# Early-fusion block on one Trainium2 core: when the softmax sums, the context and the o weights are loaded, and who scales the context

## The reference, cut to what matters

```python
def _chunk_decompose(x2d):            # chunks of 64 tokens
    ch_bias = (max + min) / 2         # per chunk and channel
    xz = xp - ch_bias
    scale = per chunk and channel, from the chunk's and the channel's max
    result = clip(round(xz / s), -8, 7) * s

attn = einsum('bqhd,bkhd->bhqk', Q, K)          # 32 heads of 16
ctx = einsum('bhqk,bkhd->bqhd', softmax(attn), V)
r2, cb2 = _chunk_decompose(ctx)
h = h + (r2 @ WO + cb2 @ o_weight.T + o_bias)
logits = layernorm(h) @ gate_w.T + gate_b       # top 2 of 8 experts
h = h + experts(layernorm(h), routing)
```

## Time and profile before

| | us |
|---|---|
| median of 3 runs | 1689.76 |
| range of the runs | 1685.97 to 1696.05 |
| profiled execution | 1692.25 |
| its span | 1690.4 |
| PE busy | 1264.5 (75%) |
| DVE busy | 1221.0 (72%) |
| ACT busy | 846.1 (50%) |
| POOL busy | 448.7 (27%) |

### The profile page before, as it was taken

How to read it: one execution, slowest core, us unless ns; L and a number is a source line. 1 busy time by engine, 2 the same in 40 slices (tenths; PEclk the granted TensorE clock), 3 DMA queues, 4 the chain that set the end, 5 groups by cost and what they waited for, 6 DMA issues and landing times. The chain is left out here.

```text
span 1690.4 us, 30070 instructions
## 1 busy us (share of the span) xinstructions
PE 1264.5 (75%) x10051; PEld 729.9 (43%) x10170; DVE 1221.0 (72%) x2030; ACT 846.1 (50%) x1748; POOL 448.7 (27%) x277
## 2 busy tenths in 40 slices
PE   0257347637989999999999886225819999999993
PEld 0245213212334444444444332003817777777772
DVE  7985999977778888888888787368474555555551
ACT  3665413321667777777777656914203444444441
POOL 4000307662234333443330003010012333333311
PEclk9968669875999999999999988556558999999997
DMA  4000206679367776677755553373229999999965
GB/s 157 0 1 4 88 0 204 217 217 208 101 177 193 198 208 190 186 194 204 212 128 100 91 140 125 76 147 126 93 106 353 314 311 306 308 306 311 308 208 143
DMA packets 115112, 294.08 MB, mean 174 GB/s; under 512 B 19971, under 2 KB 54787, under 8 KB 104641
## 3 DMA queue, kind: packets, MB, share of 16 engines
q1 hardware_dynamic: 90280, 209.27, 40.9%
q0 software_dynamic: 23712, 81.28, 18.0%
q10 hardware_dynamic: 1056, 2.79, 0.5%
HBM read 208.03 MB, written 90.32 MB: 176 GB/s over the span
## 5 line engine op out<-in xcount | busy, mean ns | idle before, releaser
L1447 ACT ACTIVATE pT<-p 128x512 f32<-128x512 f32 x800 | 422.0, 608 | 188.5 <-PE p L1340 115.3
L1412 DVE TENSOR_REDUCE mxa<-p 128x1 f32<-128x512 f32 x640 | 409.6, 682 | 104.8 <-PE p L1322 104.2
L1322 PE MATMUL p<-ks,qs 96*128 96x512 bf16 x640 | 254.4, 401 | 49.0 <-DMA vs<-d_v 31.0
L1340 PE MATMUL p<-qs,ks 128*128 128x512 bf16 x560 | 216.3, 387 | 30.4 <-DMA qs<-nmT 18.5
L1358 PE MATMUL p<-pT,vs 128*32 128x128 f32 (+1 forms) x2560 | 207.3, 442 | 1.4 <-ACT pT L1447 1.4
L2083 POOL DMA_INDIRECT d_acc<-yo,slot_row x47 | 74.6, 1587 | 268.1 <-DVE yo L2231 249.4
L2113 PE MATMUL p<-x,w 128*128 128x256 bf16 (+1 forms) x1728 | 145.5, 246 | 0.0
L2113 PEld LDWEIGHTS p<-x,w 128*128 128x128 bf16 x1728 | 133.6, 98 | 13.8
L1358 PEld LDWEIGHTS p<-pT,vs 128*32 128x32 f32 x2560 | 67.1, 109 | 153.4 <-issue 109.4
L1322 PEld LDWEIGHTS p<-ks,qs 96*128 96x128 bf16 x640 | 62.3, 98 | 153.7 <-DVE mxa L1412 58.9
L1290 POOL CAST xT<-xT 128x2048 bf16<-128x2048 f32 x24 | 45.3, 1886 | 305.5 <-PE p L1358 293.3
(11 more groups left out here) (405 smaller groups left out, 2090.4 us busy)
## 6 DMA issues: line engine op xcount, KB each, us to landing
w<-d_w SPq DMA_DIRECT2D x18, 2048.0 KB, 9.4
d_w<-xT POOLq DMA_DIRECT2D x24, 1024.0 KB, 6.5
shared<-d_w SPq DMA_DIRECT2D x10, 2048.0 KB, 7.8
w<-d_w SPq DMA_DIRECT2D x18, 1024.0 KB, 10.9
xT<-in_w1T POOLq DMA_DIRECT2D x16, 1024.0 KB, 10.7
qs<-d_q SPq DMA_DIRECT2D x192, 80.0 KB, 3.6
ks<-d_k SPq DMA_DIRECT2D x192, 80.0 KB, 3.7
d_v<-xT SPq DMA_DIRECT2D x20, 512.0 KB, 4.4
```

What stands on the lines that cost most here:

```text
L1322: mm = pe.matmul(out, qs[u][0:STACK, h, q], ks[u][0:STACK, h, 0:512], start=True, stop=True)
L1340: mm = pe.matmul(out, ks[u][:, h, k], qs[u][:, h, 0:512], start=True, stop=True)
L1412: dve.tensor_reduce(mxa[u][:, h, qt:qt + 1], bank, AX.X, ALU.max, negate=True).then_inc(s_mfree, 1)
L1447: act.activation(dst, ps[:, second_bank(c, s)], ACT.Exp).then_inc(s_p, 1)
```

## The change

In `attend`, SyncE's loop is one iteration shorter and the last looped iteration is written out: the loads of the sums, contexts and inverses, and the store of the inverses, stand between its steps. The reciprocal of the sums stands behind the maxima of group 26. The o weights and the o bias are loaded in attend (`load_o`), in the space of the first q and k buffers, after the second pass of group 28. In `route`, the late reciprocal stands ahead of the quantization of batch 0, and `put_bias(0)` ahead of the load of the late inverses. ScalarE no longer scales; VectorE's `apply` does it for every batch. The order of TensorE's and VectorE's parts is changed.

```diff
+        first_q, first_k = (sb(f"{n}s0", [P, 4, T], BF16, c=middle) for n in "qk")
+        wTo = [x[:].rearrange("p h t -> p (h t)").bitcast(F32)[:, 0:IT // 2 * L].rearrange("p (i o) -> p i o", o=L)
+               for x in (first_q, first_k)]
+        bias_o = sb("bias_o", [EARLY * (T // CHUNK), L], c=middle)
+        def load_o(sp):
+            rows = a["o_wT"].rearrange("(i p) o -> p i o", p=P)
+            for k in range(2):
+                sp.dma_start(wTo[k], rows[:, k * IT // 2:(k + 1) * IT // 2]).then_inc(s_oin, 16)
+            sp.dma_start(bias_o[:], a["L0_attn_o_bias"].partition_broadcast(EARLY * (T // CHUNK))).then_inc(s_oin, 16)
...
-            with sp.Fori(0, NI - 1) as i:
+            def step(i, c):
+                store(i, c - 1)
+                sp.wait_ge(s_s, U2 * num(i, c))
+                sp.wait_ge(s_pv, KT * num(i, c) + 1)
+                load(i, c + R - 1)
+
+            with sp.Fori(0, NI - 2) as i:
                 for c in range(1, R + 1):
-                    store(i, c - 1)
-                    sp.wait_ge(s_s, U2 * num(i, c))
-                    sp.wait_ge(s_pv, KT * num(i, c) + 1)
-                    load(i, c + R - 1)
+                    step(i, c)
...
-            for u in range(2):
-                sp.wait_ge(s_wst[u], 16 * 3 * EXP_N // 2)
-                sp.wait_ge(s_ost[u], 8 * EARLY * HEADS // GH + 1)
-            sp.dma_start(sums[0:EARLY * HEADS], heads[0:EARLY * HEADS, HD]).then_inc(s_sumin, 16)
-            for b in range(EARLY):
-                load_context(sp, b)
-            sp.wait_ge(s_rs, 1)
-            sp.dma_start(d_sum[0:EARLY * HEADS], sums[0:EARLY * HEADS]).then_inc(s_rout, 16)
-            sp.wait_ge(s_rout, 16)
-            for b in range(2):
-                load_inverses(sp, b)
+            for c in range(1, R + 1):
+                step(NI - 2, c)
+                if c == 1:
+                    for u in range(2):
+                        sp.wait_ge(s_ost[u], 8 * EARLY * HEADS // GH + 1)
+                    sp.dma_start(sums[0:EARLY * HEADS], heads[0:EARLY * HEADS, HD]).then_inc(s_sumin, 16)
+                elif c == 2:
+                    sp.wait_ge(s_rs, 1)
+                    sp.dma_start(d_sum[0:EARLY * HEADS], sums[0:EARLY * HEADS]).then_inc(s_rout, 16)
+                    for u in range(2):
+                        sp.wait_ge(s_wst[u], 16 * 3 * EXP_N // 2)
+                    load_context(sp, 0)
+                elif c == 3:
+                    sp.wait_ge(s_rout, 16)
+                    load_inverses(sp, 0)
+                    load_context(sp, 1)
+                    load_inverses(sp, 1)
+                else:
+                    load_context(sp, 2)
+                    sp.wait_ge(s_den, 1)
+                    load_inverses(sp, 2)
             for c in range(1, R + 1):
                 store(NI - 1, c - 1)
                 if c == 1:
-                    sp.wait_ge(s_den, 1)
-                    load_inverses(sp, 2)
+                    sp.wait_ge(s_s, U2 * num(NI - 1, 1))
+                    load_o(sp)
...
-            with dve.Fori(0, NI - 1) as i:
+            with dve.Fori(0, NI - 2) as i:
                 for c in range(R):
                     maxima(i, c)
             for c in range(R):
-                maxima(NI - 1, c)
-                if c == 1:
+                maxima(NI - 2, c)
+                if c == 2:
                     dve.wait_ge(s_sumin, 16)
                     dve.reciprocal(sums[0:EARLY * HEADS], sums[0:EARLY * HEADS]).then_inc(s_rs, 1)
+            for c in range(R):
+                maxima(NI - 1, c)
...
             store_late_inverses(sp)
+            put_bias(0)
             sp.wait_ge(s_rout, 16 + 16 * LATE_PARTS)
             load_inverses(sp, EARLY)
-            put_bias(0)
...
             centre(1)
-            scale(1)
             centre(2)
-            scale(2)
             deviations(0)
             centre(3)
-            scale(3)
-            copy_turned(0)
...
             rows(1)
+            gates(0)
             rows(2)
-            gates(0)
+            gates(1)
             rows(3)
-            gates(1)
             gates(2)
             gates(3)
...
             def quantized(b):
                 q, k = group(b)
-                at = q.columns(k)
-                flat = xT[:, b].rearrange("p i t -> p (i t)")
-                dve.wait_ge(s_scaled[b], 1)
+                dve.wait_ge(s_centred[b], 1)
                 if b >= 2:
                     dve.wait_ge(s_omm, COMPS * (b - 1))
-                chain(dve.tensor_scalar(flat, flat, MAGIC, QMAX, ALU.subtract, ALU.min))
-                dve.tensor_tensor(q.chunks(qF[:, b % 2]), q.chunks(xT[:, b]), q.spread(q.F[:, :, at]), ALU.mult).then_inc(s_q, 1)
+                q.apply(dve, chain, k, xT[:, b], qF[:, b % 2], s_q)
...
-            chain(dve.memset(magic[:], MAGIC))
             prepare(0, quant, range(EARLY))
+            dve.wait_ge(s_sumin, 16 + 16 * LATE_PARTS)
+            dve.reciprocal(late[:], late[:]).then_inc(s_rs, 1)
             dve.wait_ge(s_centred[0], 1)
             quant.apply(dve, chain, 0, xT[:, 0], qF[:, 0], s_q)
-            dve.wait_ge(s_sumin, 16 + 16 * LATE_PARTS)
-            dve.reciprocal(late[:], late[:]).then_inc(s_rs, 1)
             residual(0)
+            variances(0)
             dve.wait_ge(s_ctx[EARLY], 16 * 2 * IT)
             chain(dve.tensor_tensor(xT[:, EARLY], xT[:, EARLY], den[:, EARLY % 2], ALU.mult))
             last.extremes(dve, chain, 0, xT[:, EARLY])
+            normed(0)
             dve.wait_ge(last.bias_ready, 1)
             prepare(1, last, [EARLY])
-            variances(0)
             quantized(1)
             residual(1)
+            quantized(2)
             variances(1)
-            normed(0)
-            quantized(2)
+            normed(1)
             residual(2)
+            quantized(3)
             variances(2)
-            normed(1)
-            quantized(3)
+            normed(2)
             residual(3)
             variances(3)
-            normed(2)
             normed(3)
```

More of the change, by code:

```diff
@@ L172, in early_fusion_kernel @@
         heads = d_o.rearrange("g (h r) t -> (g h) r t", r=32)
+        first_q, first_k = (sb(f"{n}s0", [P, 4, T], BF16, c=middle) for n in "qk")
+        wTo = [x[:].rearrange("p h t -> p (h t)").bitcast(F32)[:, 0:IT // 2 * L].rearrange("p (i o) -> p i o", o=L)
+               for x in (first_q, first_k)]
+        bias_o = sb("bias_o", [EARLY * (T // CHUNK), L], c=middle)
+        s_oin = ctx.enter_context(nc.semaphore("o_inputs_in"))
+        def load_o(sp):
[3 more added lines that the diff above has]
+            sp.dma_start(bias_o[:], a["L0_attn_o_bias"].partition_broadcast(EARLY * (T // CHUNK))).then_inc(s_oin, 16)
         def load_late_sums(sp):
@@ L856, in apply, with round @@
     def apply(self, dve, chain, b, x, out, done):
+        x4 = self.chunks(x)
+        chain(dve.tensor_tensor(x4, x4, self.spread(self.s[:, :, self.columns(b)]), ALU.mult))
+        self.round(dve, chain, b, x, out, done)
+    def round(self, dve, chain, b, x, out, done):
         at = self.columns(b)
@@ L860, in apply @@
         flat = x.rearrange("p i t -> p (i t)")
-        chain(dve.tensor_tensor(x4, x4, self.spread(self.s[:, :, at]), ALU.mult))
         chain(dve.tensor_scalar(flat, flat, MAGIC, MAGIC, ALU.add, ALU.subtract))
@@ L1143, in attend @@
     d_w, xT4, den, quant, s_ctx, s_den, s_centred = (g[n] for n in ("d_w", "xT4", "den", "quant", "s_ctx", "s_den", "s_centred"))
-    load_late_sums = g["load_late_sums"]
+    load_late_sums, load_o = g["load_late_sums"], g["load_o"]
     GH = 4
@@ L1170, in sem @@
             return ctx.enter_context(nc.semaphore(name))
-        qs = [sb(f"qs{u}", [P, GH, T], BF16) for u in range(R)]
-        ks = [sb(f"ks{u}", [P, GH, T], BF16) for u in range(R)]
+        qs = [g["first_q"]] + [sb(f"qs{u}", [P, GH, T], BF16) for u in range(1, R)]
+        ks = [g["first_k"]] + [sb(f"ks{u}", [P, GH, T], BF16) for u in range(1, R)]
         vs = [sb(f"vs{u}", [P, KT, GH * 32]) for u in range(R)]
@@ L1524, in route @@
     s_ctx, s_sumin, s_rs, s_rout, s_centred = (g[n] for n in ("s_ctx", "s_sumin", "s_rs", "s_rout", "s_centred"))
-    load_inverses, store_late_inverses = g["load_inverses"], g["store_late_inverses"]
+    load_inverses, store_late_inverses, wTo, bias, s_oin = (g[n] for n in (
+        "load_inverses", "store_late_inverses", "wTo", "bias_o", "s_oin"))
     LATE_PARTS = T // LATE_COLS
@@ L1538, in route @@
         qF = sb("qF4", [P, 2, IT, T], BF16)
-        wTo = sb("wTo", [P, IT, L])
-        bias = sb("bias_o", [NE, L])
         Bt = [sb("Bt_early", [NE, L]), sb("Bt_last", [NB, L])]
-        magic = sb("magic4", [P, 1])
         gtok = sb("gtok4", [P, TILES])
@@ L1588, in route @@
         s_unit = sem("unit_experts_ready")
-        s_in, s_rin = sem("o_inputs_in"), sem("router_inputs_in")
+        s_rin = sem("router_inputs_in")
         c_dve = sem("p4_dve_chain")
```

(22 more changed lines are left out.)

## The result

| | before | after |
|---|---|---|
| median, us | 1691.78 (4 runs) | 1669.68 (4 runs) |
| range, us | 1685.97 to 1696.05 | 1667.11 to 1670.49 |
| profiled execution, its span | 1692.25, 1690.4 | 1667.11, 1665.3 |

Forecast were 1673 and the range 1658 to 1687.

A forecast was written before the change was run, and what follows sets the result against it. The prediction took TensorE's chain through the expert stage, fed by VectorE's routing, as the bound. Attention +10, t0 -24 and rest of the block -5 made -19 us: 1692.25 to 1673.3, said as 1673, range 1658 to 1687.

The forecast's parts named there:

- attention: Segment from the end of group 26's maxima to the route block: forecast 10 us longer.
- t0: VectorE's first addition into hs; from the route block's start to it, forecast 24 us less, bounds 18 to 28.
- The sums' stall: In attention, VectorE's wait for the sums moves from behind group 29's maxima to group 26's: 0 us.
- Rival B: In attention, the sums come before VectorE asks, giving up to 8.2 us: 1665 us, chance 0.06.
- Load 31: Last q/k load in attention, queued behind inverses and context 1; TensorE stands 8 to 11 us, 10 taken, bounds 0 and 23.
- Rival A: In attention, load 31 comes in time on idle engines with smaller spill: 1663 us, chance 0.17.
- Bt_early: In routing, VectorE starts it 8.5 us earlier, with o weights and bias loaded ahead; bounds 8 to 9.5.
- The first addition into hs: In routing, the accumulation's 11.4 us grows by 0 to 6, 4 taken, with batch 3's inverses running beside it.
- Rival D: In routing, GpSimd's descriptors or shared engines hold the accumulation 12 us more: 1685 us, chance 0.12.
- idle of 8 to 11 us: Sign of a right forecast: TensorE or VectorE idles on a DMA at the start of group 31's scores.
- VectorE's scaling: In routing, VectorE's scaling adds 2.95 us for each of three batches, 8.9 us on the bound engine.
- The order of parts: From t0 to the logits, reordered quantize, residual, normed and gates, scaling included: 5 us less, bounds 0 to 8.

The follow-up runs named there:

- a3: Changed kernel with the early reciprocal of the sums behind the maxima of group 27 instead of 26: 1662.27 us, ratio 0.9819 to before.
- a1: Changed kernel with attention's old schedule of loads and sums' reciprocal, o weights still loaded in attention: 1668.43 us, ratio 0.9865 to before.
- a2: Kernel before with only attention's new schedule, routing as before and o weights loaded there: 1693.22 us, ratio 0.9998 to before.
- b4: Changed kernel with inverses 0 and 1 and contexts 1 and 2 issued behind load 31: 1673.96 us, ratio 0.9891 to before.
- c0: Changed kernel with GpSimd's three products waiting for VectorE's joined maxima of groups 29, 30 and 31: 1670.06 us, ratio 0.9872 to before.
- b1: Changed kernel with batch 3's inverses loaded only after the first two accumulations into hs have landed: 1675.31 us, ratio 0.9911 to before.
- c1: Changed kernel, batch 3's inverses behind the first two hs accumulations, GpSimd's accumulations of batches 1 to 3 behind those inverses: 1662.76 us, ratio 0.9826.
- b2: Changed kernel with Bt_early written behind the late inverses again: 1673.01 us, ratio 0.9896 to before.
- b3: Changed kernel with ScalarE scaling batches 1 to 3 again, in the new order of parts: 1661.04 us, ratio 0.9826 to before.

## Why the prediction was right, and where a term was not

The time came out in the range, 3 us below the forecast, and the sum of the three segments as forecast. Two terms were off in opposite directions, attention by 4.7 us and t0 by 5.2, and they cancelled: that the sum is so close is luck.

**The sums' stall: right.** It moved and did not shrink (8.06 us), as the equal phase of store and maxima said. Rival B is refuted by the row, though a3 shows that it was one line away.

**Load 31: the mechanism right, the size wrong.** This is the first step that failed: "It ends at about C26 + 41. Load 31 waits behind them and lands some 8 to 11 us later". The copy of group 26 began at 952.98. GpSimd's second product, released by inverses 1, starts at 992.89 = C26 + 39.9, so the transfers ahead ended about when forecast. But load 31's v landed at 982.48 + 16.9 = 999.4, C26 + 46.4: 6.5 us behind them, and not 8 to 11. And it was needed later than C26 + 41.5, at about C28 + 4 = 998.3 (the copy of 28 at 994.34), C26 + 45.4, since the groups between had slipped too. The stall was 1.38 us where 10 stood in the sum. That load 31 did not pass is plain from the landing: v took 4.5 and 4.8 us in the last two loads of before, 5.3 and 5.0 in loads 28 and 30 of after, and 16.9 behind the inverses. The Trainium skill, "DMA: Bandwidth & Descriptors", section on queues, rings and completion order, says that each engine takes its own ring in order; this landing agrees. Part of the lateness came before the queue: inverses 1 held SyncE for 8.42 us, so store 27 was issued at 975.01, 2.5 us behind the end of its copy. Rival A was nearly right that load 31 costs little, but for the wrong reason: nothing passed on idle engines.

**The rest of attention's slip: not foreseen.** The segment grew by 5.3 us (a1 and a2 give 4.0 and 5.9). The steps between the ends of the `nm` additions tell where, held against 18.5 to 18.9 us for a step of before without a stall. In after the step with the stall is 1.1 us shorter than before's; the steps to groups 28, 29, 30 and 31 are longer by 0.6, 2.6, 1.4 and 3.1; and from group 31 to the block it is 1.3 shorter. The 2.6 us are the held addition of group 29, the 1.4 are TensorE's wait for load 31, and 1.5 of the 3.1 are the held addition of group 31; the rest stays open. Taking away the wait (b4) or the held additions (c0) gave nothing: in b4 an addition was held for 3.80 us elsewhere, and in c0 the late row of maxima took its place.

**Bt_early: right.** From the block's first instruction to its start it was 18.1 us and is 8.5: 9.5 us earlier, forecast 8.5 with bounds of 8 to 9.5.

**The first addition into hs: the second step that failed**, "0 to 6 us, I take 4". The pieces of this segment, worked out from the rows of both:

| piece, us | before | after | difference |
|---|---|---|---|
| block to Bt_early done | 18.8 | 9.2 | -9.5 |
| to the late reciprocal done | 8.4 | 1.1 | -7.3 |
| to GpSimd's start | 15.8 | 3.8 | -12.0 |
| to t0 | 11.4 | 21.5 | +10.1 |

The first three are as forecast or better (Bt_early landed at 1068.25, 2.0 us after its issue; the forecast had 1.8). The fourth was taken at +4 and is +10.1, outside its bounds. b1 shows the cause: without inverses beside it the accumulation is 10.8 us. I had taken 7.5 us for a batch of inverses and bounded the sharing below that. By c1 they take 10.6 us alone, and the accumulation beside them is longer by 10.7, as much as if the one stood behind the other. b2 gives the consequence: moving `put_bias` ahead of the inverses has gained nothing (34.63 against 35.53 us). The 12.0 and the 10.1 us are one exchange; what the change earned at t0 are the o weights (9.5) and the late reciprocal (7.3). This split is read from the rows; neither of the two was taken back alone. Rival D named the shared engines as a cause of a late accumulation, and that is what b1 shows. Its price was 12 us more than my 4; measured are 6.1 more. Of the signs, the wait for hs "from 25 to about 10" failed with this step (15.16), and the "idle of 8 to 11 us" with the first.

**VectorE's scaling: right,** 8.9 forecast and 9.2 measured by b3. ScalarE's passes had been hidden, so this part of the change costs its whole length.

**The order of parts: right,** -5 with the scaling in it, -5.6 measured. The waits for rows before residual(2) and (3) are gone. gates(2) took 1183.28 - 1175.50 = 7.8 us, below its bound, and gates(3) 12.7 to the logits, where 9 to 12.6 and 12.6 were forecast. The clock fell again when only the gates were left:

```profile
1175.00:1178.00 3.00, 2.76 (x19) 2.25 (x18) 2.92 (x5) 1.07 (x2) 0.00 (x0) 0.86 0.00 0
1184.00:1187.00 3.00, 3.00 (x15) 2.78 (x14) 1.00 (x3) 1.17 (x2) 0.00 (x0) 0.50 1.02 375
```

## What to carry to other kernels

Moving a wait for a DMA keeps the wait if the distance in the code stays the same: a3 put one group of other work between issue and use, and had some 8 us of the whole time for one line. Two transfers that are needed one after the other are best issued one after the other, over all queues that carry them. Putting the urgent one ahead on its own queue gained nothing here while the next one ran beside it (b2), holding back only one of the others moved the wait (b1), and ordering all three took it away (c1). Work on the bound engine had its full price though it relieved another engine (b3), and where several small delays stood side by side, taking away one showed nothing (b4, c0).

## What the runs showed of the hardware that was not expected

A VectorE addition of two operands in SBUF stands still until a running GpSimd product ends: 2.80 us instead of 0.18 in group 29, ending at 979.13 where the product ended at 979.09. The addition of group 31 and both in b4 end within 0.04 us of a product too, and in c0, where no product runs beside them, all take 0.18. The trace of before had it already: two additions of 128x40 (before's L815) took 1.26 and 3.55 us instead of 0.20 and ended within 0.06 us of a product. The Trainium skill, "SBUF — State Buffer", section on the two separate sides, says that a VectorE operation with two SBUF inputs and a GpSimd operation that reads SBUF need the same port pair, which the one that starts first has for its whole instruction while the other is blocked; these rows agree.

The accumulation of one batch (two DMAs) into SBUF takes 10.8 us alone (b1, c1) and 21.5 us beside one batch of inverses, though the two are issued by different engines.
